# Moving the value products of a query-tile pair behind the next scores in the last batch of a decoder-layer kernel

## The chip, the cores and the metric

One core of one Trainium2 chip runs the whole kernel in one launch. The metric is the device time of that launch in microseconds (us), the median of several executions. The names of the engines in the profile are PE (TensorE, matmuls and transposes), PEld (its weight loads), DVE (VectorE), ACT (ScalarE), POOL (GpSimd) and SP (the engine that only issues transfers here).

## The reference, cut to what matters

```python
x = x + attn(layernorm(x), Wq, bq, Wk, bk, Wv, bv, Wo, bo)   # x: 4 batches x 512 tokens x 512
x = x + experts(layernorm(x), token_ids, ctx)                # 4 experts, each token to one
x = x + ffn(layernorm(x), w_gate, w_up, w_down, ln_weight)   # quantized activations, ternary weights

def attn(h, ...):            # 16 heads of 32, window of 128 keys back, 4 sink keys always seen
    q, k, v = h @ Wq.T + bq, h @ Wk.T + bk, h @ Wv.T + bv
    scores = q @ k.T * 32 ** -0.5
    banned = (j >= 4) & (j < i - 128)      # i query, j key; keys ahead of i are NOT banned
    probs = softmax(where(banned, -inf, scores))
    return (probs @ v) @ Wo.T + bo
```

The change lies in `probs @ v` ("the value products") of the last of the four batches. The computed values stay the same.

## The kernel before, in words

The attention phase works on units (b, g, qt): batch b, a group g of four heads, and one of four query tiles qt of 128 tokens. Group 0 of a batch is worked off at the end of the batch before it, so the last batch (b = 3) has the twelve units g = 1 to 3. Every engine runs its own program, an order written out by hand, and semaphores join them.

For one unit:

- PE, `scores(b, g, qt)` (L948, L956): the products of queries and keys of four heads, in three terms (high and low halves), plus a mask, into the four banks of `s_ps`. There is only one set of these banks, so the scores of a unit wait until ACT has taken all exponentials of the unit before.
- DVE, `maxima` (L724): the row maxima, in two halves of two heads.
- ACT, `exps` (L548): four exponentials with their row sums, the first two after the first half of the maxima, into the buffer `weights[qt]`.
- PE, `transpose_slot(b, g, qt, k)`, k = 0 to 3 (L976; the four sink keys L972; in unit 3 the widened inverse sums L969): the weights are transposed block by block into two banks of `pT_ps`; ACT copies slots 0 and 2 back (L560), DVE slots 1 and 3 (L745, L742). Slot 2 can be transposed when ACT has copied slot 0, slot 3 when DVE has copied slot 1.
- PE, `attend_pair(b, g, pair)` (L998, with L990 for the sinks): for a pair of query tiles (0 and 1, or 2 and 3) the value products, 32 or 24 matmuls and 2 more, into the one bank `pv_ps`.
- DVE, `attn_of(b, g)` (L736): `pv_ps` times the inverse sums, after both pairs of a group; POOL splits the result into a high and a low part (L412, L415), which the output projection needs.

PE's order within a unit is: the scores of the next unit, transposes 0 and 1, a "side" product (projections of Q, K, V or of the output, L889), transposes 2 and 3, and in units 1 and 3 the value products of the pair that is now complete. In the last batch only group 1 has side products (O2, O3, Q3, K3); units (2, 0) to (3, 1) have none, and `o_begun(0)`, the first part of the last output projection, comes in unit (3, 2).

The buffers of both pairs overlap in the memory of `probs`: `weights[3]` lies over a part of `weights[1]`. So the exponentials of unit (g, 3) may not be written before the value products of pair 0 of the group have read `weights[1]`, and those of unit (g + 1, 1) not before the products of pair 2 have read `weights[3]`. Before the change this follows from PE's order, as the scores of those units stand behind the value products.

In what follows a unit is named by (g, qt), all of b = 3, and T0 to T3 are its four sets of transposes.

Of the kernel before, what the change touches and what calls it, by code (L numbers as in the profile page):

```python
# [11 lines left out]
BATCH, SEQ, D = 4, 512, 512  # L12
# [3 lines left out]
HG = HEADS // GH  # L16
# [43 lines left out]
def attention_phase(nc, io, x1, x2, slot_tokens, dense_tokens, sh):  # L60
# [7 lines left out]
    with ExitStack() as ctx:  # L68
# [123 lines left out]
        def width(qt):  # L192
            sink, kts, _ = blocks(qt)
            return SINKS * sink + P * len(kts)
# [21 lines left out]
        def units_before(b, g, qt):  # L216
            return b * GU + g * TT + qt
# [29 lines left out]
        def projected(b, g, qt):  # L247
            name = PROJECTED[g].split()[qt]
            return None if name == "-" or (g and not taken(b, name)) else name
# [9 lines left out]

        def in_key_order(keys):  # L260
            return keys.rearrange("p (u n) -> p u n", u=2)[:, :, SINKS:]

        def key_columns(keys, rows, g, qt):
            if qt < 2:
# [238 lines left out]
        def scalar_program(act):  # L503
# [39 lines left out]

            def exps(b, g, qt, s):
                act.wait_ge(max_ready, units_before(b, g, qt) * 2 + s + 1)
                at = BAND - width(qt) if qt >= 2 else 0
                for h in (2 * s, 2 * s + 1):
                    nc.scalar.activation(weights[qt][:, h, at:at + width(qt)], s_ps[:, h, 0:width(qt)], ACT.Exp,  # L548
                                         bias=neg_max[:, qt % 2, h:h + 1],
                                         accum_out=sums[:, g % 2, qt, h:h + 1]).then_inc(exp_done, 1)  # L550
# [57 lines left out]
        def vector_program(dve):  # L608
# [123 lines left out]

            def attn_of(b, g):
                dve.wait_ge(slot_copied[1], copies_before(b, g, TT - 1, SLOTS - 1) + 1)
                dve.wait_ge(heads_done, b * HG + g + 1)
                nc.vector.tensor_tensor(norm[:], pv_ps[:], norm[:], ALU.mult).then_inc(attn_ready, 1)  # L736

            def copy_slot(b, g, qt, k):
                slot = slots_of(qt)[k]
                dve.wait_ge(slot_transposed, slots_before(b, g, qt, k) + 1)  # L740
                if slot == "rinv":
                    nc.vector.tensor_copy(norm[:], pT_ps[:, 1, :]).then_inc(slot_copied[1], 1)  # L742
                else:
                    a, z = columns(qt, slot)
                    nc.vector.tensor_copy(weights[qt][:, :, a:z], pT_ps[:, 1, :].rearrange("p (h n) -> p h n", h=GH))\  # L745
                        .then_inc(slot_copied[1], 1)

            def unit(b, g, qt, last):
                nxt = (g, qt + 1) if qt + 1 < TT else (g + 1, 0)
                more = not (last and nxt == (HG, 0))  # L750
                coming = b + 1 if g == 0 else b + 2
                prepare = g in (0, HG) and coming < BATCH
                name = turned(b, g, qt - 1) if qt else turned(b, g - 1, TT - 1)
                if name:
                    x_lo(b, int(name[1]), side_ps[:])
                if qt == TT - 1:
                    invert(b, g)
                if (g, qt) == (HG, 0):
                    attn_of(b, g - 1)
                if more:  # L760
                    maxima(b, *nxt, 0)
                    maxima(b, *nxt, 1)
                if qt == 0 and 0 < g < HG:
                    attn_of(b, g - 1)
                if prepare and qt in (1, 2):
                    for t in (2 * qt - 2, 2 * qt - 1):
                        stats_of(coming, t)
                if qt >= 2:
                    a, z = columns(qt, "sink")
                    dve.wait_ge(exp_done, units_before(b, g, qt) * GH + GH)  # L770
                    nc.vector.tensor_reduce(sinks[:], weights[qt][:, :, a:z].unsqueeze(3), AX.X, ALU.max).then_inc(sinks_gathered, 1)
                copy_slot(b, g, qt, 1)
                if prepare and qt in (1, 2):
                    dve.wait_ge(stats_step, coming * TT + 2 * qt)
                    for t in (2 * qt - 2, 2 * qt - 1):
                        variance_of(coming, t)
                name = projected(b, g, qt)
                if name and name[0] == "V":
                    v_of(b if g else -1, int(name[1]), side_ps[:], v_next if g else v_sb)
                if name and name[0] == "O":  # L780
                    dve.wait_ge(side_done, nth(b, name))
                    x1_of(batch_of(b, name), int(name[1]), side_ps[:], side_left)
                copy_slot(b, g, qt, 3)
                if name and name[0] in "QK":
                    qk_lo(heads_of(g, name), name[0], nth_in(b, g, name, "XQK"))
                if prepare and qt == TT - 1:
                    for t in (0, 1):
                        normalize(coming, t)
                if not last and (g, qt) == (1, 0):
                    for t in (2, 3):  # L790
                        normalize(b + 1, t)
                if last and (g, qt) == (HG - 1, TT - 1):

                    e = SPLIT_ORDER[-1]
                    dve.wait_ge(c_split, 2 * EXPERTS - 1)
                    nc.vector.tensor_tensor(place(sh["w_lo"], e), v_next[:], place(sh["w_hi"], e).bitcast(F32), ALU.subtract)\
                        .then_inc(c_split, 1)
                if (g, qt) == (HG, 0):

                    dve.wait_ge(side_left, nth(b, "V3"))  # L800
                    nc.vector.tensor_copy(v_sb[:], v_next[:]).then_inc(v_moved, 1)
# [82 lines left out]
        def tensor_program(pe):  # L884
# [75 lines left out]
            def transpose_slot(b, g, qt, k):  # L960
                slot = slots_of(qt)[k]
                if copies_before(b, g, qt, k):
                    pe.wait_ge(slot_copied[k % 2], copies_before(b, g, qt, k))
                if k == 0:
                    pe.wait_ge(exp_done, units_before(b, g, qt) * GH + GH)
                if slot == "rinv":
                    pe.wait_ge(rinv_widened, b * HG + g + 1)
                    for t in range(TT):
                        last = nc.tensor.transpose(pT_ps[:, 1, place_of(t)], norm[:, t * P:t * P + P], ident[:])  # L969
                elif slot == "sink":  # L970
                    pe.wait_ge(sinks_gathered, 2 * (b * HG + g) + qt - 1)
                    last = nc.tensor.transpose(pT_ps[0:GH * SINKS, 0, 0:P], sinks[:].rearrange("p h n -> p (h n)"), ident[:])  # L972
                else:
                    a, z = columns(qt, slot)
                    for h in range(GH):
                        last = nc.tensor.transpose(pT_ps[:, k % 2, h * P:h * P + P], weights[qt][:, h, a:z], ident[:])  # L976
                last.then_inc(slot_transposed, 1)
# [24 lines left out]
            def attend_pair(b, g, pair):  # L1002
                if pair == 0 and g:
                    pe.wait_ge(attn_ready, b * HG + g)
                    if g == HG:
                        pe.wait_ge(v_moved, b + 1)
                slots = [2, 1, 3, "sink"] if pair else slots_of(pair)
                for n, slot in enumerate(slots):
                    last = attend(b, g, pair, slot, n == 0, n + 1 == len(slots))
                if pair:  # L1010
                    last.then_inc(heads_done, 1)

            def o_begun(t):
                if t == 0:
# [4 lines left out]
            def unit(b, g, qt, last):  # L1019
                nxt = (g, qt + 1) if qt + 1 < TT else (g + 1, 0)  # L1020
                if not (last and nxt == (HG, 0)):
                    scores(b, *nxt)
                transpose_slot(b, g, qt, 0)
                transpose_slot(b, g, qt, 1)
                name = projected(b, g, qt)
                if name:
                    side(b, nth_in(b, g, name), name)
                if last and g == HG - 1 and qt >= 2:
                    o_begun(qt - 2)
                transpose_slot(b, g, qt, 2)  # L1030
                transpose_slot(b, g, qt, 3)
                if last and (g, qt) == (HG - 1, TT - 1):
                    o_begun(2)
                if qt % 2:
                    attend_pair(b, g, qt - 1)
                name = turned(b, g, qt)
                if name:
                    side(b, nth(b, name), name)
# [986 lines left out]
```

## Time and profile before

| | us |
|---|---|
| median of three runs | 785.86 (783.3, 785.86, 787.12) |
| the profiled execution, its own time | 789.38 |
| its span in the trace | 787.3 |
| PE busy | 735.5 (93%) |
| DVE busy | 587.4 (75%) |
| ACT busy | 473.1 (60%) |
| POOL busy | 331.2 (42%) |
| units (1, 0) to (3, 3) and the output projection of the last batch | 378.9 to 457 |

The profiled execution took 2.1 us beyond its span, and 3.5 us more than the median of the runs. Times of rows are counted from the start of the span. The busy share is a mean over stages with different limits: attention reaches to about 457 us, the experts and the feed-forward part follow. The granted clock is given as a share of full speed: 1.00 is 2.4 GHz and 0.50 is 1.2 GHz.

### The profile page before, as it was taken

The page shows a single profiled execution, that of the slowest core. Times are in us where ns is not written, and L with a number is a line of the kernel's source. Part 1 is how long each engine was busy: PE and PEld are TensorE (multiplying, and loading weights), DVE is VectorE, ACT ScalarE, POOL GpSimd, SP SyncE. Part 2 cuts the span into 40 slices and gives each one's busy share as a digit, 9 for nine tenths or more (in the row PEclk, how much of TensorE's full clock was granted, in tenths as well). Part 3 has the DMA queues.
Part 4 walks back from the last instruction along what each step waited for, and adds up shares of the span by engine and source line. Part 5 has one row for each costly group of instructions (what it writes and reads, how often), then busy time and mean ns, then how long its engine had stood idle before and what let it go on. Part 6 is the DMA issues. An engine that isn't in the chain of part 4 may idle for free.

```text
span 787.3 us, 14189 instructions
## 1 busy us (share of the span) xinstructions
PE 735.5 (93%) x5167; PEld 512.7 (65%) x5184; DVE 587.4 (75%) x1099; ACT 473.1 (60%) x1028; POOL 331.2 (42%) x329
## 2 busy tenths in 40 slices
PE   5988999999999999999987989999998999999993
PEld 4866777777777776777764777888874444444441
DVE  6986866886667866766665548878888999999882
ACT  4565666766676665766666314444455787667761
POOL 2011205213242134254553544445546677777661
PEclk9998999999999999999999999999999999999997
DMA  9300012214130322314311356555430233333231
GB/s 314 115 1 27 28 40 95 92 44 151 40 107 29 108 85 77 108 31 153 129 40 55 54 198 258 182 197 201 140 126 25 54 88 87 94 95 102 73 92 42
DMA packets 55474, 78.33 MB, mean 99 GB/s; under 512 B 36335, under 2 KB 38383, under 8 KB 53680
## 3 DMA queue, kind: packets, MB, share of 16 engines
q1 hardware_dynamic: 46336, 51.99, 20.6%
q0 software_dynamic: 8784, 24.93, 9.8%
q8 instruction: 43, 0.70, 0.4%
q10 hardware_dynamic: 288, 0.52, 0.2%
q14 instruction: 23, 0.19, 0.1%
HBM read 56.92 MB, written 17.59 MB: 95 GB/s over the span
## 4 chain that ended last, share of the span: by engine, by line
PE 62%; DVE 20%; issue 8%; ACT 5%; POOL 2%; DMA 1%; another core or an unknown queue 0%; ACTq 0%; SPq 0%; POOLq 0%; DVEq 0%
PE side_ps L889 17%; PE pT_ps L976 10%; PE e_z_ps L1528 7%; PE y_ps L1528 7%; PE pv_ps L998 5%; PE s_ps L948 5%; DVE h L1784 4%; ACT hq L1739 2%; DVE neg_max L724 2%; DVE hw_max L1800 2%; DVE hq_big L1831 2%; PE s_ps L956 2%; PE pT_ps L889 1%; DVE probs L745 1%; ACT f_gate L1746 1%
## 5 line engine op out<-in xcount | busy, mean ns | idle before, releaser
L548 ACT ACTIVATE probs<-s_ps,neg_max 128x512 f32<-128x512 f32 (+2 forms) x256 | 152.5, 611 | 17.9 <-DVE neg_max L724 16.4
L724 DVE TENSOR_REDUCE neg_max<-s_ps 128x2 f32<-128x1024 f32 (+2 forms) x128 | 124.6, 1015 | 36.1 <-PE s_ps L956 35.0
L976 PE MATMUL pT_ps<-ident,probs 128*128 128x128 f32 x832 | 116.5, 282 | 7.8 <-DVE probs L745 7.0
L560 ACT ACTIVATE probs<-pT_ps 128x512 f32<-128x512 f32 x96 | 57.5, 599 | 98.7 <-PE pT_ps L976 97.3
L976 PEld LDWEIGHTS pT_ps<-ident,probs 128*128 128x128 f32 x832 | 95.1, 145 | 23.0 <-DVE probs L745 9.7
L745 DVE COPY probs<-pT_ps 128x512 f32<-128x512 f32 x112 | 76.8, 685 | 39.1 <-PE pT_ps L976 36.2
L1695 POOL TENSOR_TENSOR xg_own<-h,ln_w_sb 128x512 f32<-128x512 f32 x63 | 81.9, 1308 | 37.9 <-DVE h L1784 37.8
L889 PE MATMUL side_ps<-w_hi 128*128 128x512 f32 x172 | 71.0, 413 | 0.0
L412 POOL TENSOR_TENSOR aT_hi<-norm,one_col 128x512 fp32r<-128x512 f32 x15 | 15.6, 1041 | 126.6 <-DVE norm L736 88.4
L889 PE MATMUL side_ps<-w_hi,w_lo 128*128 128x512 f32 x172 | 67.5, 392 | 0.0
L889 PE MATMUL side_ps<-w_lo,w_hi 128*128 128x512 f32 x172 | 67.0, 390 | 0.0
L1739 ACT ACTIVATE hq<-hq_big,minus_offset 128x1024 bf16<-128x1024 f16 x30 | 32.9, 1142 | 37.3 <-DVE hq_big L1831 37.3
L998 PE MATMUL pv_ps<-probs,v_sb 128*32 128x256 f32 (+1 forms) x896 | 54.0, 378 | 1.4 <-DVE probs L745 0.9
L1905 PE MATMUL y_ps<-w_tern,hqT 128*128 128x512 bf16 x210 | 54.5, 379 | 0.7
L404 POOL TENSOR_TENSOR norm<-rinv,one_col 128x512 f32<-128x512 f32 x16 | 16.7, 1041 | 86.0 <-DVE rinv L731 86.0
L548 ACT ACTIVATION_READ_ACCUMULATOR probs<-s_ps,neg_max 128x1 f32 x256 | 52.8, 206 | 0.0
L1657 PE MATMUL e_xT_ps<-w_tern,xqT_home 128*128 128x512 bf16 x126 | 32.6, 378 | 7.3 <-DVE h L1784 6.5
L1800 DVE TENSOR_REDUCE hw_max<-xg_own 128x1 f32<-128x1024 f32 x32 | 38.7, 1209 | 0.1
L998 PEld LDWEIGHTS pv_ps<-probs,v_sb 128*32 128x32 f32 x896 | 25.7, 112 | 20.0 <-issue 8.0
L889 PEld LDWEIGHTS side_ps<-w_hi,w_lo 128*128 128x128 f32 x172 | 32.3, 188 | 7.4
L1905 PEld LDWEIGHTS y_ps<-w_tern,hqT 128*128 128x128 bf16 x224 | 21.4, 98 | 23.4
L889 PEld LDWEIGHTS side_ps<-w_hi 128*128 128x128 f32 x172 | 32.4, 188 | 5.9 <-DVE k_lo L648 0.4
(290 smaller groups left out, 1779.4 us busy)
## 6 DMA issues: line engine op xcount, KB each, us to landing
w_piece<-w_ffn SPq DMA_DIRECT2D x24, 512.0 KB
w_stage<-w_ffn SPq DMA_DIRECT2D x12, 1024.0 KB
xres<-x POOLq DMA_DIRECT2D x4, 1024.0 KB, 6.4
xn<-x SPq DMA_DIRECT2D x3, 1024.0 KB
x<-xres POOLq DMA_DIRECT2D x3, 1024.0 KB, 4.8
xn<-c SPq DMA_DIRECT2D x2, 1024.0 KB, 5.1
v_next<-c SPq DMA_DIRECT2D x2, 1024.0 KB, 7.5
xn<-x SPq DMA_DIRECT2D x4, 256.0 KB, 3.4
```

Of the source, the lines that this page charges most:

```text
L548: nc.scalar.activation(weights[qt][:, h, at:at + width(qt)], s_ps[:, h, 0:width(qt)], ACT.Exp, bias=neg_max[:, qt % 2, h:h + 1], accum_out ...
L560: nc.scalar.activation(out, turned_p, ACT.Identity).then_inc(slot_copied[0], 1)
L724: nc.vector.tensor_reduce(neg_max[:, qt % 2, 2 * s:2 * s + 2], s_ps[:, 2 * s:2 * s + 2, 0:width(qt)], AX.X, ALU.max, negate=True).then_inc ...
L745: nc.vector.tensor_copy(weights[qt][:, :, a:z], pT_ps[:, 1, :].rearrange("p (h n) -> p h n", h=GH))\
L889: last = nc.tensor.matmul(out, lt, r, start=(first and n == 0), stop=(final and n == len(terms) - 1))
L976: last = nc.tensor.transpose(pT_ps[:, k % 2, h * P:h * P + P], weights[qt][:, h, a:z], ident[:])
L998: last = nc.tensor.matmul(pv_ps[HD * h:HD * h + HD, to], v_sb[:, slot, f:f + HD], p, start=first, stop=final, tile_position=(0, HD * h))
L1528: last = nc.tensor.matmul(out, lt[:, k, :], r[:, at, :], start=(n == 0), stop=(n == 3 * DK - 1))
L1695: nc.gpsimd.tensor_tensor(hw[:, t % 2, c, :], h[:, t % 2, c, :], ln_w[:, c * CHK:c * CHK + CHK], ALU.mult)\
L1739: nc.scalar.activation(hq[:, cols], hq_code[:, cols], ACT.Identity, bias=minus_offset[:]).then_inc(hq_packed, 1)
L1800: nc.vector.tensor_reduce(hw_max[:, i, n:n + 1], flat(hw, i)[:, n * HALF:n * HALF + HALF], AX.X, ALU.max, apply_absolute_value=True).then_ ...
L1905: last = nc.tensor.matmul(sums_of(t), hqT[:, t % 2, k, :], down_w[:, k, :], start=(k == 0), stop=(k == FK - 1))
```

## The change

In the last batch, for groups 1 to 3, the value products of a pair no longer stand at the end of the unit that completes the pair. They stand one unit later: behind the scores of the unit after that and behind T0 and T1. This holds for five pairs: (1, pair 0), (1, pair 2), (2, pair 0), (2, pair 2) and (3, pair 0). The pair (3, pair 2) stays at the end. Two waits are added on ACT, since PE's order no longer protects the overlapping buffers; DVE takes `attn_of` of groups 1 and 2 behind the copy of slot 1. `heads_done` now counts both pairs, in all batches.

```diff
+        def values_late(b, g, pair):
+            return b == BATCH - 1 and 1 <= g < HG and (g, pair) != (HG - 1, 2)
+
+        def values_of(b, g, pair):
+            return 2 * (b * HG + g) + (2 if pair else 1)
...
             def exps(b, g, qt, s):
                 act.wait_ge(max_ready, units_before(b, g, qt) * 2 + s + 1)
+                if s == 0 and qt == 3 and values_late(b, g, 0):
+                    act.wait_ge(heads_done, values_of(b, g, 0))
+                if s == 0 and qt == 1 and g and values_late(b, g - 1, 2):
+                    act.wait_ge(heads_done, values_of(b, g - 1, 2))
...
-                dve.wait_ge(heads_done, b * HG + g + 1)
+                dve.wait_ge(heads_done, values_of(b, g, 2))
...
-                if qt == 0 and 0 < g < HG:
+                follows_late = qt == 0 and 0 < g < HG and values_late(b, g - 1, 2)
+                if qt == 0 and 0 < g < HG and not follows_late:
                     attn_of(b, g - 1)
...
                 copy_slot(b, g, qt, 1)
+                if follows_late:
+                    attn_of(b, g - 1)
...
-                if pair:
-                    last.then_inc(heads_done, 1)
+                last.then_inc(heads_done, 1)
...
                 transpose_slot(b, g, qt, 0)
                 transpose_slot(b, g, qt, 1)
+                if qt == 2 and values_late(b, g, 0):
+                    attend_pair(b, g, 0)
+                if qt == 0 and g and values_late(b, g - 1, 2):
+                    attend_pair(b, g - 1, 2)
...
-                if qt % 2:
+                if qt % 2 and not values_late(b, g, qt - 1):
                     attend_pair(b, g, qt - 1)
```

## Rows read from the trace of the kernel before

**Rows 1.** The page: busy time and share of the span by engine.
```profile
PE 735.5 (93%) x5167; PEld 512.7 (65%) x5184; DVE 587.4 (75%) x1099; ACT 473.1 (60%) x1028; POOL 331.2 (42%) x329
```
**Rows 2.** Busy time by stretch: length, engines' busy us (instructions), granted clock, DMA.
```profile
378.90:401.30 22.40, 22.40 (x189) 17.65 (x186) 15.12 (x22) 13.81 (x39) 7.50 (x6) 1.00 0.29 97
...
409.40:412.80 3.40, 3.40 (x18) 2.81 (x15) 2.51 (x3) 2.44 (x8) 3.40 (x2) 0.51 0.00 0
...
419.60:423.00 3.40, 1.56 (x17) 0.97 (x10) 3.03 (x4) 2.44 (x6) 0.84 (x1) 1.00 0.00 0
423.00:426.40 3.40, 3.40 (x32) 1.77 (x32) 0.69 (x1) 1.59 (x6) 0.00 (x0) 0.50 0.03 5
...
433.20:436.60 3.40, 3.40 (x18) 2.82 (x16) 2.49 (x3) 2.42 (x8) 3.40 (x2) 0.50 0.00 0
```
**Rows 3.** Chain that ended last, in order of time: start, length, what.
```profile
391.96 0.88 PE pT_ps L976 x8
...
401.35 1.22 PE pv_ps L998 x24
...
403.19 0.69 PE s_ps L948 x8
...
409.47 3.51 PE pT_ps L976 x16
412.98 1.95 PE pv_ps L998 x32
414.93 0.56 PE s_ps L948 x8
415.49 0.33 PE s_ps L956 x4
...
418.74 0.14 issue
418.88 1.00 PE s_ps L948 x9
...
419.90 2.35 DVE neg_max L724 x2
...
422.98 1.11 PE pT_ps L969 x4
424.09 2.29 PE pv_ps L998 x24
```
**Rows 4.** Timeline of ACT: start, length, line, out<-in, idle before and releaser.
```profile
401.38 0.21 ACT L548 ACTIVATION_READ_ACCUMULATOR probs<-s_ps,neg_max 128x1 f32 x1
...
405.39 0.69 ACT L548 ACTIVATE probs<-s_ps,neg_max 128x512 f32<-128x512 f32 x1
...
410.36 0.60 ACT L560 ACTIVATE probs<-pT_ps 128x512 f32<-128x512 f32 x1 [1.70 <-PE pT_ps L976]
410.86 0.58 ACT L548 ACTIVATE probs<-s_ps,neg_max 128x388 f32<-128x388 f32 x1
...
413.00 0.22 ACT L548 ACTIVATION_READ_ACCUMULATOR probs<-s_ps,neg_max 128x1 f32 x1
...
416.79 0.47 ACT L548 ACTIVATE probs<-s_ps,neg_max 128x260 f32<-128x260 f32 x1
...
421.16 0.69 ACT L548 ACTIVATE probs<-s_ps,neg_max 128x512 f32<-128x512 f32 x1
...
429.24 0.69 ACT L548 ACTIVATE probs<-s_ps,neg_max 128x512 f32<-128x512 f32 x1
```
**Rows 5.** Timeline of PE: the same columns.
```profile
407.74 0.66 PE L976 MATMUL pT_ps<-ident,probs 128*128 128x128 f32 x4 [1.75 <-DVE probs L745]
408.32 0.45 PE L948 MATMUL s_ps<-k_hi,q_hi 32*128 32x388 f32 x4
...
438.67 0.39 PE L948 MATMUL s_ps<-k_hi,q_hi 32*128 32x260 f32 x4
```
**Rows 6.** Timeline of POOL: the same columns.
```profile
432.13 1.28 POOL L415 TENSOR_TENSOR aT_lo<-norm,aT_hi 128x512 fp32r<-128x512 f32 x1
```

## The prediction, on record before the result

> **What bounds the kernel now.** I read the page first: PE is busy for 93% of the span [rows 1], so a gain can only come where PE pauses or runs slow. Then I cut the last batch into stretches [rows 2]. Until 401.3 us, with the side products of group 1, PE has no pause: reordering its work there gains nothing. From group 2 on there are no side products, and PE pauses (1.56 us busy out of 3.40 in one stretch). In three stretches the granted clock is 0.50, that is 1.2 GHz. Each comes after a passage in which PE paused, the first after a pause of 1.75 us [rows 2, 5].
>
> Then I read the chain of waits [rows 3] beside ACT's timeline [rows 4] for the round from unit (2, 1) to (3, 1). It is a ring: scores on PE, first half of the maxima on DVE, four exponentials on ACT, and then the next scores, since the score banks exist once. Its first exponentials start at 405.39 in one round and at 429.24 in the next: 23.85 us. The value products interrupt the ring twice in it: 412.98 to 414.93 (pair 0) and from 424.09 (pair 2), where 24 matmuls take 2.29 us at the low clock against 1.22 us at 401.35 at the full one. The question is what the ring becomes when these products stand elsewhere.
>
> **The links of the ring**, from row starts at full clock [rows 3 to 5]:
> - From the first exponential of a unit to the next scores: 512 columns, 408.32 - 405.39 = 2.93; 260 columns, 418.88 - 416.79 = 2.09; 388 columns, the last sum read ends at 413.22, 2.36 after 410.86, plus the hop of 0.14: 2.50.
> - Scores alone: 260 columns, 414.93 to 415.82, 0.9; when they start from a pause 0.07 more (0.96). 512 columns without a mask 1.00, with a mask about 1.25 from a pause (four mask matmuls add 0.2 to 0.3). 388 columns 409.47 - 408.32 = 1.15.
> - From scores of 512 columns to the exponentials: 421.16 - 419.90 = 1.26. T0 and T1 together: 0.88. Value products: 403.19 - 401.35 = 1.84 for pair 2, 1.95 for pair 0 (1.9 used).
> - Where ACT's copy of slot 0 stands between (units with 388 columns): T0 0.44 and copy 0.50 behind the scores.
>
> **What is removed and added.** Nothing is computed less. Removed from the place before the scores are the products of five pairs. What they are moved past are the scores (0.9 to 1.25) and T0 and T1 (0.88); they issue no transfers, and SP's and POOL's queues aren't touched. The catch is the added wait on ACT: the exponentials of (g, 3) and (g + 1, 1) must wait for the same products. The old path at such a place is products, scores, maxima (or copy), exponentials. The new one is scores, T0, T1, products, exponentials. The products stay on the path; the maxima go off it, and T0 and T1 come on it. Behind the waiting exponentials on ACT stand the copy of slot 2, on which the last transposes depend, and behind their end the next scores, the ring itself. So:
>
> - Place (1, pair 0): inside the stretch without pauses. Exponentials of (1, 3) wait for products that end where they began by work before. 0.
> - Place (1, pair 2): old 405.39. New: the scores of (2, 1) can't start when PE is free at 401.35, since the exponentials of (2, 0) end at 401.59; plus the hop, 401.74. Then 1.25 + 0.88 + 1.84 + 0.02: exponentials at about 405.75. Late by 0.36.
> - (2, 1): scores at 405.75 + 2.93 = 408.68, end 409.83, T0 and copy 0.97: exponentials at 410.82 (old 410.86, where T0 and T1 ran at the low clock).
> - Place (2, pair 0): scores of (2, 3) at 410.82 + 2.50 = 413.32 instead of 414.93. They are early by 1.6. But then 0.96 + 0.88 + 1.9 + 0.02 = 3.76 gives exponentials at 417.08, old 416.79: late by 0.3.
> - (3, 0): 417.08 + 2.09 + 1.02 + 1.26 = 421.45, old 421.16.
> - Place (2, pair 2): scores of (3, 1) at 421.45 + 2.93 = 424.38, plus 1.25 + 0.88 + 1.84 + 0.02 = 3.99: 428.37 against the old 429.24. Early by 0.87, and only because the old place ran at the low clock (0.55 in L969, 1.07 in the 24 matmuls).
> - Group 3: 428.37 + 2.93 + 2.12 (1.15 + 0.97, scores, T0 and copy) + 2.50: scores of (3, 3) at 435.92, old 438.67 [rows 5], early by 2.75; the products (1.9) now follow them before `o_begun(0)`. PE is early by about 0.8 there, and from that point on its work is dense and the same, so 0.8 is what arrives at the end of attention.
>
> Sum with PE at full clock throughout: -0.8 us. The old round lost about 2.4 to the low clock (0.55 and 1.07 in (2, 3), some 0.4 each at the first transposes of (2, 1) and (3, 1)); against an old ring at full clock the new one would be slower by about 1.6. The moved order costs a little by itself.
>
> The small parts. `attn_of` behind DVE's copy of slot 1 lets T3 of (2, 0) start earlier (old pause 1.75 us [rows 5]), but scores could start at 408.32 anyway, when ACT was done: 0, covered by the exponentials. POOL's split, ending at 433.41 [rows 6], moves with `attn_of` and is wanted by `o_begun(0)` only after the products of (3, pair 0), near 439.7: covered by over 5 us. The waits on ACT: no row shows a second wait alone; from 0 to the hop of 0.14 [rows 3] at four binding places, so 0 to 0.6; I take 0.1, as the trace's hops between engines that are ready are mostly a few hundredths. The sixteen added semaphore increments are 0: the scores at 403.19 follow directly on products that already carry one [rows 3]. The Trainium skill ("TensorE: Matmul & The Clock Gate", "The cost: per-tile semaphore tail") gives about 26 ns for each increment; an estimate by that page is 16 x 0.026 = 0.4 us if every one lay on the path, and the row at 403.19 shows none of it.
>
> **The clock in the new order.** The new order still has pauses, worked out from the same links: about 1.6 us before the scores of (2, 2), in place of 1.75; about 1.5 and 0.6 around the sink transposes of (2, 3) and 0.65 before the scores of (3, 1), where before 1.56 us of work out of 3.40 preceded a fall; about 2 us before the scores of (3, 2). So falls will follow as before. What they hit is different: behind the pauses of (2, 3) stand scores, T0, T1 and products in a row, 3.97 us, all on the path. A low stretch was 3.4 us long in each of three cases [rows 2] and does half the work, so it costs up to 1.7; for a part cover I take 1.4. The falls at (2, 1) and (3, 1) hit T0 in front of a copy: 0.43 each (T0 once more). The low estimate for all is 0, the high one three times 1.7. I take the fall at (2, 3) and one of the others: 1.4 + 0.4. The Trainium skill (the same page, "Part 1: The HAM clock gate") says that the point at which the clock changes varies between runs of one kernel; the three times from 783.3 to 787.12 don't contradict that, and no run here shows its cause.
>
> **Sum**: -0.8 + 0.1 + 1.4 + 0.4 = +1.1 us. The profiled execution's own 789.38 would become 790.5. It lies 3.5 above the median of the runs, so I carry the difference over: 785.86 + 1.1, about 787.0. Half a per cent, 3.9 us, is what a measurement of this kernel can tell from no change, so this is no change.
>
> **The rivals.**
> 1. Break-even as summed, with falls of the clock in old or new places: between -0.8 and +2.7 (a second place at 1.7). Chance 0.72.
> 2. PE stays warmer: no fall in the last batch, and PE's work overlaps more than my links say (up to 0.3 at four places): -0.8 - 1.2 = -2.0, 783.9. For it: the densest work is pushed together. Against it: the sum of pauses hardly shrinks. Chance 0.15.
> 3. The products go under the maxima entirely, the added wait never binds: four places (all but the first) at 1.84 to 1.95, 7.6 us faster, 778.3. It decides if T0, T1 and the products, 2.72 us, fit into the 1.26 us of the maxima. By the rows they don't. Chance 0.05; this is where "faster" has its chance.
> 4. Slower: the low clock covers the new row of scores, transposes and products at each of the three places after a pause, 3 x 1.7 = 5.1, and the increments and waits cost too: -0.8 + 5.1 + 0.6 = +4.9, 790.8. It decides from three such falls on. For it: the path through PE at such a place is now 3.97 us instead of products and scores of 2.8. Against it: in front of (2, 2)'s and (3, 2)'s units the pauses are shorter or the fall comes one unit too early. Chance 0.08.
>
> The range takes rivals 1, 2 and most of 4, and adds the scatter of a median of few runs (the three lie 3.8 us apart): 783.5 to 790.0. The chances by the bound of half a per cent: faster 0.05, same 0.87, slower 0.08.
>
> **What the profile after would show.** Right: exponentials of (2, 1), (2, 3), (3, 1) and (3, 3) released by PE's value products and no longer by the maxima; the maxima of those units done 1.5 us before; scores of (2, 3) and (3, 3) starting 1.6 to 2.8 us earlier while the exponentials behind them don't; the round from (2, 1) to (3, 1) between 22.5 and 24.5 us. Wrong: if exponentials follow the maxima directly, if the round is below 21.5, or if a pause of PE appears before 401 us. A difference above 4 us with an unchanged round would mean that the cause lies outside the last batch.

## The result, and the profile after

The changed kernel takes 787.02 us, the kernel before 785.26 us, both medians of 20 runs. The ratio of all runs but one is 1.0026, with a 95% interval from 1.0014 to 1.0039: 2.0 us slower, between 1.1 and 3.1 (the two medians alone differ by 1.8). One run of the changed kernel took 1477.61 us, at a granted clock on record as 1.000; it is left out of the ratio, and its cause is open. By the bound of half a per cent this is no change; by its own interval it is a small loss. Forecast was 787.0.

The profiled execution took 786.93 us, with a span of 785.0, and is so 2.3 us shorter in its span than that of the kernel before. That says nothing of the change: the first exponential of (1, 2), before which PE has the same order in both programs, starts at 382.43 here and started 3.2 us later there. A part of these 3.2 us is a further fall of the clock far ahead of the change: from 57.0 to 61.5 us the granted clock was 0.62 on the mean before and 1.00 after; both have one near 68 us. From that exponential to the first sum of the output projection out of the score banks on DVE (`x1_of`, the row `xres<-s_ps`) it is 452.73 - 382.43 = 70.30 us after, and was 69.51 us before. I call this length **the stage** below; both ends lie outside what the change moves. Behind the stage all profiled executions of this document but one (e7) agree within 0.3 us, 332.0 to 332.3; ahead of it they scatter from 382.1 to 385.6.

The page of after, engines' busy time, against [rows 1]; PE is less busy because its clock fell less often in this execution:

```profile
PE 730.8 (93%) x5167; PEld 509.5 (65%) x5184; DVE 587.1 (75%) x1099; ACT 473.4 (60%) x1028; POOL 330.7 (42%) x329
```

The timeline of ACT of after, the first exponentials of the four units behind a moved pair (the columns of [rows 4]):

```profile
402.75 0.69 ACT L559 ACTIVATE probs<-s_ps,neg_max 128x512 f32<-128x512 f32 x1 [1.74 <-PE pv_ps L1004]
...
413.94 0.48 ACT L559 ACTIVATE probs<-s_ps,neg_max 128x260 f32<-128x260 f32 x1 [1.79 <-PE pv_ps L1012]
...
426.81 0.69 ACT L559 ACTIVATE probs<-s_ps,neg_max 128x512 f32<-128x512 f32 x1 [2.66 <-PE pv_ps L1004]
...
438.01 0.48 ACT L559 ACTIVATE probs<-s_ps,neg_max 128x260 f32<-128x260 f32 x1 [1.79 <-PE pv_ps L1012]
```

All four are now released by PE's value products: (2, 1), (2, 3), (3, 1) and (3, 3). This is the added wait, and it binds each time. The round from (2, 1) to (3, 1) takes 426.81 - 402.75 = 24.06 us, where [rows 4] give 23.85.

The chain that ended last, of after, over the same places as [rows 3]:

```profile
382.34 2.80 PE side_ps L903 x12
...
387.78 1.86 PE pv_ps L1012 x32
389.64 2.94 PE side_ps L903 x12
...
398.63 0.96 PE s_ps L962 x11
399.59 0.33 PE s_ps L970 x4
399.92 0.88 PE pT_ps L990 x8
400.81 1.22 PE pv_ps L1012 x24
402.02 0.64 PE pv_ps L1004 x2
...
410.11 0.63 PE s_ps L962 x11
410.74 0.33 PE s_ps L970 x4
411.07 0.88 PE pT_ps L990 x8
411.95 1.91 PE pv_ps L1012 x32
...
421.14 0.99 PE s_ps L962 x9
422.14 0.52 PE s_ps L970 x4
422.66 1.71 PE pT_ps L990 x8
424.37 1.72 PE pv_ps L1012 x24
426.09 0.64 PE pv_ps L1004 x2
...
426.81 2.79 ACT probs L559 x8
```

Three times the same row of work stands in front of the exponentials: scores, two sets of transposes, value products, all on PE. At (2, 3) it is 413.94 - 410.11 = 3.83 us; 3.76 was worked out. At (2, 1) it is 402.75 - 398.63 = 4.12 us; the same row at (3, 1), from 421.14, takes 5.67 us, because the transposes took 1.71 instead of 0.88, the 24 matmuls 1.72 instead of 1.22 and the mask's matmuls 0.52 instead of 0.33. The stretches of after say why (the columns of [rows 2]); in the last batch of this execution the clock fell once, right behind a passage in which PE was busy 1.78 us out of 3.40:

```profile
418.60:422.00 3.40, 1.78 (x17) 1.00 (x17) 2.17 (x4) 3.14 (x10) 0.00 (x0) 0.99 0.00 0
422.00:425.40 3.40, 3.40 (x32) 2.53 (x32) 2.91 (x3) 0.60 (x1) 0.00 (x0) 0.51 0.02 5
```

So the two profiled executions can't be set against each other as they are: before had three falls in the last batch, after one. What both programs would take without falls is what the experiments had to show.

### The profile page after: what moved, and what is told of

Same layout as the page of the kernel before. It is cut to its first block, busy times and chain, and to the rows that moved or that the text cites. A ratio compares the mean times of both kernels' runs of the same rounds, so it can differ in the third digit from the quotient of the medians.

```text
span 785.0 us, 14194 instructions
## 1 busy us (share of the span) xinstructions
PE 730.8 (93%) x5167; PEld 509.5 (65%) x5184; DVE 587.1 (75%) x1099; ACT 473.4 (60%) x1028; POOL 330.7 (42%) x329
## 4 chain that ended last, share of the span: by engine, by line
PE 61%; DVE 16%; ACT 10%; issue 8%; POOL 2%; DMA 1%; ACTq 0%; SPq 0%; POOLq 0%; DVEq 0%
PE side_ps L903 17%; PE pT_ps L990 9%; PE e_z_ps L1545 7%; PE y_ps L1545 7%; PE pv_ps L1012 6%; PE s_ps L962 5%; DVE h L1801 3%; ACT probs L559 3%; ACT sq_junk L1771 2%; ACT hq L1756 2%; ACT f_gate L1763 2%; DVE hq_big L1848 2%; DVE neg_max L735 2%; PE s_ps L970 2%; PE pT_ps L903 1%
## 5 line engine op out<-in xcount | busy, mean ns | idle before, releaser
L990 PE MATMUL pT_ps<-ident,probs 128*128 128x128 f32 x832 | 114.4, 278 | 6.1 <-DVE probs L756 5.3
L990 PEld LDWEIGHTS pT_ps<-ident,probs 128*128 128x128 f32 x832 | 93.4, 143 | 20.9 <-DVE probs L756 7.5
L1012 PE MATMUL pv_ps<-probs,v_sb 128*32 128x256 f32 (+1 forms) x896 | 52.3, 370 | 0.0
L962 PE MATMUL s_ps<-k_hi,q_hi 32*128 32x512 f32 (+2 forms) x256 | 33.8, 456 | 6.5 <-ACT probs L559 6.5
```

The costliest lines, as they stand in the source:

```text
L962: last = nc.tensor.matmul(s_ps[:, h, 0:width(qt)], q[rows, g % HG, cols], key_columns(k, rows, g % HG, qt), start=(n == 0), stop=(n == 2 a ...
L1012: last = nc.tensor.matmul(pv_ps[HD * h:HD * h + HD, to], v_sb[:, slot, f:f + HD], p, start=first, stop=final, tile_position=(0, HD * h))
```

## The experiments

Theory 1, **the ring**: with the buffers overlapping, the exponentials wait for products that now stand behind scores, T0 and T1, so nothing leaves the path and a little is added. Rival A: the waits, the added increments and DVE's order cost the time. Rival B: only the clock's falls, which lie elsewhere in the new order, make the difference. "Extra" in the table stands for small products without use that keep PE busy; they come with e7 below.

In the table all distances are in us between first exponentials on ACT, read from the timeline of ACT as above; "falls" is the number of low stretches of PE's clock from 400 us to the end of attention in the profiled execution. A distance marked with * has at least a part of a fall in it.

| kernel | ratio to before (95%) | (2,0) to (2,1) | (2,2) to (2,3) | (3,0) to (3,1) | stage | falls |
|---|---|---|---|---|---|---|
| before | 1 | 6.58 | 5.93* | 8.08* | 69.51 | 3 |
| after | 1.0026 (1.0014 to 1.0039) | 6.96 | 6.25 | 8.50* | 70.30 | 1 |
| e1 waits only | 0.9988 (0.9976 to 1.0000) | 6.59 | 5.93* | 6.51 | 68.00 | 1 |
| e2 pair 0 late | 1.0024 (1.0010 to 1.0038) | 6.58 | 6.26 | 8.13* | 71.07 | 2 |
| e3 pair 2 late | 1.0012 (0.9999 to 1.0024) | 6.96 | 6.42* | 8.23* | 69.97 | 3 |
| e4 apart | 0.9961 (0.9946 to 0.9976) | 5.71 | 4.36 | 5.32 | 64.22 | 0 |
| e5 T1 behind | 0.9978 (0.9965 to 0.9991) | 6.52 | 5.82 | 6.52 | 67.35 | 0 |
| e6 split, shared | 0.9930 (0.9909 to 0.9951) | 6.17 | 5.14 | 5.46 | 64.45 | 0 |
| e7 after, ten extra | 1.0038 (1.0025 to 1.0052) | 6.96 | 6.25 | 6.96 | 70.08 | 0 |
| e8 apart, extra | 0.9934 (0.9912 to 0.9955) | 5.71 | 4.35 | 5.33 | 64.22 | 0 |
| e9 before, extra | 0.9979 (0.9967 to 0.9991) | 6.58 | 5.94 | 6.53 | 67.21 | 0 |
| e10 after, five extra | 0.9999 (0.9987 to 1.0011) | 6.95 | 6.26 | 6.96 | 68.78 | 0 |
| e11 split, apart | 0.9933 (0.9917 to 0.9948) | 6.20 | 4.53 | 5.47 | 64.16 | 0 |

**e1, the waits without the move.** All of the change but PE's order.

```diff
-                if qt == 2 and values_late(b, g, 0):
-                    attend_pair(b, g, 0)
-                if qt == 0 and g and values_late(b, g - 1, 2):
-                    attend_pair(b, g - 1, 2)
...
-                if qt % 2 and not values_late(b, g, qt - 1):
+                if qt % 2:
```

> PE's order is that of the kernel before; the two waits on ACT, the increment of heads_done for both pairs in all batches, and attn_of behind DVE's copy of slot 1 are those of the change. Theory 1 (the ring: what costs is the new row scores, T0, T1, value products in front of the exponentials): no difference, within 0.8 us of before. Rival A (the waits, increments and DVE's order cost the 2 us): about 2 us slower, 1.0025.

Not slower: 0.9988, that is 0.9 us faster (0 to 1.9) where at most 0.8 of difference was expected, and where no fall lies in either the distances are those of before to 0.01 us (7.31, 5.87 and 6.59 from (1, 2) on). Rival A falls. The sixteen increments, which this kernel carries, cost nothing that can be measured. The Trainium skill ("TensorE: Matmul & The Clock Gate", "The cost: per-tile semaphore tail") would allow up to 0.4 us by the prediction's estimate; the interval's upper end is 1.0000, and nothing in these runs points to such a cost, though their falls, which vary from run to run, are in the interval too. And e1 gave the first look at (3, 0) to (3, 1) in the old order without a fall: 6.51 us instead of 8.08.

**e2 and e3, one half of the move each.**

```diff
-            return b == BATCH - 1 and 1 <= g < HG and (g, pair) != (HG - 1, 2)
+            return b == BATCH - 1 and 1 <= g < HG and pair == 0          # e2
+            return b == BATCH - 1 and 1 <= g < HG - 1 and pair == 2      # e3
```

> Only the value products of pair 0 of groups 1 to 3 stand late. Theory 1: at places (2, pair 0) and (3, pair 0) the exponentials come 0.3 to 0.4 us later after the previous exponentials than in the old order at full clock, and each first product behind value products starts up to 0.2 later: +0.8 to +1.2 us in all, 1.0010 to 1.0015. In the trace the time from the first exponential of (2, 2) to that of (2, 3) is 6.25, as after. Rival A: about +1.2. Rival B (only falls of the clock make the difference): anything from -1 to +3, with every link at full clock equal to before.

> Only the value products of pair 2 of groups 1 and 2 stand late. Theory 1: +0.4 at (1, pair 2) and +0.4 at (2, pair 2), +0.8 us in all, 1.0010; from the first exponential of (3, 0) to that of (3, 1) 6.9 us at full clock and up to 8.6 with a fall in it. Rival A: about +0.8. Rival B: no fixed sign.

e2: 1.0024, more than the 1.0015 I had as the upper end, though its interval reaches below that. (2, 2) to (2, 3) is 6.26 as in after, +0.33 on the old order, and (3, 2) to (3, 3) is 6.25, with 5.93 in e1; of the places of pair 2, (2, 0) to (2, 1) is unchanged at 6.58, and the other has a fall in it as before. The runs of e2 have a median granted clock of 0.986 where those of before have 0.988, so a part of its excess may be falls. e3: 1.0012, with +0.38 at (2, 0) to (2, 1); its 6.42 at (2, 2) to (2, 3), where the old order stands, has a fall in it. The parts together (3.6 per thousand) are not distinguishable from the whole (2.6), given intervals of 1.2 to 1.4 to either side. By its distances each half loses by itself (e3's ratio alone, from 0.9999 on, doesn't show it): there is no good half that the other spoils. The profiled executions of these two had two and three falls, so their stages can't be used.

**e4, the buffers apart.** The order of after; the second pair gets its own 6 KB for each partition, and the waits on ACT, no longer needed, go.

```diff
-        probs = sb("probs", [P, 2 * GH * SEQ + GH * BAND])
+        probs = sb("probs", [P, 2 * GH * (SEQ + BAND)])
...
-                2: probs[:, 2 * GH * (SEQ - BAND // 2):].rearrange("p (u h n) -> p u h n", u=2, h=GH)}
+                2: probs[:, 2 * GH * SEQ:].rearrange("p (u h n) -> p u h n", u=2, h=GH)}
...
-                if s == 0 and qt == 3 and values_late(b, g, 0):
-                    act.wait_ge(heads_done, values_of(b, g, 0))
-                if s == 0 and qt == 1 and g and values_late(b, g - 1, 2):
-                    act.wait_ge(heads_done, values_of(b, g - 1, 2))
```

> The order of the change, but the buffers of the two pairs no longer overlap (6 KB more for each partition), so the two waits on ACT are gone: nothing makes the exponentials wait for the value products. Theory 1: the products leave the ring at four places; exponentials follow the maxima or the copy of slot 0 again; about 3 us faster than before (0.996), 5 us faster than after. Rival A: at most 1 us from after. Rival B: near after. If PE itself is the bound of the last batch, it is not faster than before either.

0.9961, 3.1 us faster than before and 5 faster than after, as expected. This is the experiment that decides: the same order on PE and DVE gains as soon as the exponentials need not wait. In its chain around (3, 1) the maxima stand in front of the exponentials again, and no value products stand in the ring between them:

```profile
418.49 0.97 PE s_ps L958 x11
419.46 0.23 PE s_ps L966 x2
419.69 0.02 issue
419.71 1.24 DVE neg_max L731
420.95 0.02 issue
420.97 2.79 ACT probs L555 x8
423.77 0.04 issue
423.81 0.80 PE s_ps L958 x9
```

The gain is 3 us and not the 7.6 of rival 3, and the distances show why. At four places it is 6.58 - 5.71, twice 5.93 - 4.36 (the second from (3, 2) to (3, 3), 4.35) and 6.52 - 5.32 (e9 for the old order without a fall), 5.2 us in all, since part of the old products already ran before the ring was ready for the next scores. About 0.2 is lost around group 1, where PE has no pauses, and 0.25 at (2, 3) to (3, 0). And at the end 2 us are given back: the exponentials of (3, 3) start at 430.26, but PE's first product of the output projection only at 431.96, 1.7 behind them, where it starts 0.3 ahead of them before. PE has become the bound there.

**e5, T1 behind the products.**

```diff
                 transpose_slot(b, g, qt, 0)
-                transpose_slot(b, g, qt, 1)
                 if qt == 2 and values_late(b, g, 0):
                     attend_pair(b, g, 0)
                 if qt == 0 and g and values_late(b, g - 1, 2):
                     attend_pair(b, g - 1, 2)
+                transpose_slot(b, g, qt, 1)
```

> As after, but the value products stand between T0 and T1 instead of behind both. Theory 1: one set of four transposes (0.44 us) leaves the ring at each of the four places: from the first exponential of (2, 2) to that of (2, 3) 5.8 instead of 6.25, from (2, 0) to (2, 1) 6.5 instead of 6.96; in all 1.8 us faster than after, 1.0003 of before. Rival B (the clock alone): no fixed change of these distances at full clock.

The distances came out as worked out, 5.82 and 6.52: 0.43 and 0.44 less than after. The chain of e5 at (2, 3) has one set of transposes left in front of the products:

```profile
409.61 0.64 PE s_ps L962 x10
410.24 0.33 PE s_ps L970 x4
410.57 0.44 PE pT_ps L990 x4
411.01 1.91 PE pv_ps L1012 x32
...
413.00 1.96 ACT probs L559 x8
```

By its stage (67.35) this kernel is near the old order without falls (67.21, e9). The measured 0.9978 is better than the 1.0003 expected, by about the 1.6 us that falls cost the kernel before (e9). Its profiled execution had no fall in the last batch, and the granted clocks of its twelve runs say that this was no luck: their median is 0.9925, near the 0.992 and 0.993 of the filled kernels e9 and e10, where before and after have 0.988. Why this order has fewer falls isn't shown.

**e7, e9 and e10, the clock held.** Extra products of the identity with itself (the expectations call them transposes) into the unused side bank, results not used, in PE's pauses, in after with ten (e7) and five (e10) for each pause, in before with five or two (e9). The comments in the diff are not in the code; where they name e9, its line differs.

```diff
+            def fill(n):
+                pe.wait_ge(side_left, nth(BATCH - 1, "K3"))
+                for _ in range(n):
+                    nc.tensor.matmul(side_ps[:, 0:P], ident[:], ident[:], start=True, stop=True)
...
+                if last and (g, qt) in ((2, 0), (2, 2), (3, 0)):   # e7, e10: behind T3; e9: (2, 0) and (3, 0) behind T2
+                    fill(10)                                       # e10: 5
...
+                if last and (g, qt) == (2, 3):                     # behind T1; e9: also fill(2) at (2, 2)
+                    fill(10)                                       # e10: 5
```

> As after, with ten extra transposes of the identity (results unused) in each of four pauses of PE in units (2, 0), (2, 2), (2, 3) and (3, 0), so that the clock has less reason to fall. Theory 1: no fall in the last batch; from (3, 0) to (3, 1) 6.9 us instead of 8.5, the other distances as after; 1 to 2 us faster than after, 1.000 to 1.0015 of before. If the distances other than (3, 0) to (3, 1) shrink, the price of the order itself is a matter of the clock and theory 1 is wrong.

> The kernel before, with extra transposes of the identity into the unused side bank in PE's pauses of the last batch: five behind T2 of (2, 0) and (3, 0), two behind T1 of (2, 2), five behind T1 of (2, 3), short enough to end within the pauses. Theory 1: no fall of the clock in the last batch; all distances at their full-clock lengths (6.59, 4.94, 5.93, 4.37, 6.51, 4.94, 5.93 us from the first exponential of (2, 0) on); 1 to 2 us faster than before, 0.998. If the falls cost nothing on the path, 1.000.

> As e7 with five extra transposes for each pause instead of ten, which ran past the pauses there. Theory 1: no fall, distances 6.96, 4.94, 6.25, 4.37, 6.96, 4.94, 6.25 us; 1.7 to 2.0 us slower than e9, about 1.000 of before. Rival B (the clock alone makes the difference of the change): the same time as e9.

e7 missed its time: 1.0038 instead of about 1.001. The clock indeed never fell in its last batch and (3, 0) to (3, 1) is 6.96, but I had sized the filling wrongly: each of the ten is two records of 0.12 us, so a row of ten takes 2.4 us, longer than any pause. The timeline of PE of e7, with the scores of (2, 2) directly behind:

```profile
405.12 2.40 PE L1029 MATMUL side_ps<-ident 128*128 128x128 f32 x20
407.45 0.45 PE L962 MATMUL s_ps<-k_hi,q_hi 32*128 32x388 f32 x4
```

That cost 0.48 at (2, 1) to (2, 2), 0.6 at (2, 3) to (3, 0) and 0.25 at (3, 1) to (3, 2), 1.3 in all. It isn't the whole miss: e7 is 3.1 us slower than e10 by the ratios. Its profiled execution also has 335.7 us behind the stage instead of 332.0 to 332.3, with a fall of the clock near 770 us; why is open, and so is whether its other runs have that. With five, e10 has after's distances everywhere, 68.78 us of stage; e9 has before's, 67.21 (two of its other distances are 0.1 longer than in e1, 5.05 for 4.94, which is its filling). From the timelines of ACT, (3, 0) and (3, 1) in e9 and then in e10:

```profile
417.99 0.69 ACT L548 ACTIVATE probs<-s_ps,neg_max 128x512 f32<-128x512 f32 x1
...
424.52 0.69 ACT L548 ACTIVATE probs<-s_ps,neg_max 128x512 f32<-128x512 f32 x1
```

```profile
417.96 0.69 ACT L559 ACTIVATE probs<-s_ps,neg_max 128x512 f32<-128x512 f32 x1
...
424.92 0.69 ACT L559 ACTIVATE probs<-s_ps,neg_max 128x512 f32<-128x512 f32 x1 [1.74 <-PE pv_ps L1004]
```

The order alone, at full clock, costs 68.78 - 67.21 = 1.57 us by the trace, and 0.9999 - 0.9979, 1.6 us, by the runs. Without e9's own 0.2 us of filling it would be about 1.8 by the trace. Rival B is out as the sole cause. The runs give the price of the falls too, each with an error of about 1 us or more: before loses 1.6 us to them (e9 against before, 0.7 to 2.6), after about 2.1 (0.9999 against 1.0026).

The granted clock, on record for every run as a mean over its span, counts the falls where no trace was kept. One low stretch of 3.4 us lowers it by about 0.0022 (an estimate: half of 3.41 us out of 785). The medians are 0.988 in 22 runs of before and 0.988 in the 19 of after, 0.992 in e9 and 0.993 in e10. So an ordinary run of either order has about two low stretches more than the filled kernels, and neither order has clearly more than the other.

**e6, e8 and e11, versions that beat both.** e6 keeps the shared buffers and cuts each pair's products by slots, so that those whose weights are ready go into PE's pauses; e8 is e4 with the filling in its one pause; e11 is e6 with e4's buffers.

```diff
+                if qt == 2 and values_late(b, g, 0):            # behind T0
+                    attend_pair(b, g, 0, slice(2, 4))
+                if qt == 0 and g and values_late(b, g - 1, 2):
+                    attend_pair(b, g - 1, 2, slice(3, 4))
...
+                if qt == 3 and g > 1 and values_late(b, g, 2):  # behind T1
+                    attend_pair(b, g, 2, slice(0, 2))
...
+                if qt == 1 and values_late(b, g, 0):            # behind T2
+                    attend_pair(b, g, 0, slice(0, 1))
...
+                if qt == 1 and values_late(b, g, 0):            # behind T3
+                    attend_pair(b, g, 0, slice(1, 2))
+                if qt == 3 and values_late(b, g, 2):
+                    attend_pair(b, g, 2, slice(2 if g > 1 else 0, 3))
```

> The buffers still overlap, and the value products are cut up by slots: those whose weights are copied early go into PE's pauses (slot 0 of pair 0 between T2 and T3 of unit 1, slot 1 behind T3; slots 2 and 1 of pair 2 behind T1 of unit 3, slot 3 behind T3), the rest stands behind the next scores and T0 (slots 2 and 3 of pair 0; for pair 2 only the sinks, so no wait is left there). (1, pair 0) stands as before. Theory 1: from (2, 2) to (2, 3) 4.9 us, from (3, 0) to (3, 1) 5.5, from (2, 0) to (2, 1) about 6.0; about 3.3 us faster than before, 0.996. If it isn't, then the count of products in front of the exponentials is not what sets the ring.

> As e4 (buffers apart, no wait on ACT), with ten extra transposes of the identity in the one pause of 1.6 us that PE still has, in unit (2, 3). Theory 1: the same distances as e4, and no fall in any run: between 0 and 1 us faster than e4, 0.995 to 0.996 of before, and less scatter.

> e6 with the buffers apart and without the last wait on ACT. Theory 1: from (2, 2) to (2, 3) 4.4 us instead of 5.14, from (3, 0) to (3, 1) as in e6; 0.8 us faster than e6, half a us faster than e4, 0.992 to 0.995 of before.

All three are at 0.993, 5.2 to 5.5 us faster than before. e6's distances were worked out as 4.9, 5.5 and 6.0 and are 5.14, 5.46 and 6.17. Its chain at (2, 3) shows eight and sixteen value products, in two parts of 0.57 and 1.04 us, where 1.9 us stood in one place:

```profile
410.06 0.57 PE pv_ps L1010 x8
410.63 0.56 PE s_ps L960 x9
411.19 0.33 PE s_ps L968 x4
411.52 0.44 PE pT_ps L988 x4
411.97 1.04 PE pv_ps L1010 x16
```

Of its 5.5 us, 2.8 are the shorter stage at full clock (67.21 - 64.45), and about 1.6 are falls that it seems to be spared; 1.1 are left over, inside the interval (3.3 us in all had been expected). That its runs are spared falls fits their median granted clock of 0.992. e8's stage is e4's to 0.01 us; its intervals and e4's overlap, so whether the filling helped is not shown, though the median granted clock is 0.992 in e8 and 0.990 in e4: e4's profiled execution without a fall was better than its ordinary ones. e11 was expected 0.8 us under e6 and is the same: its stage is only 0.3 shorter, though (2, 2) to (2, 3) fell to 4.53. PE is near its bound at the end of the batch in both (busy for 15.79 of the 16 us from 430 to 446 in either), and the distances won ahead of it are lost there. e6, which needs no memory, is the one to keep.

## Why the prediction was right

**The path, link by link.** The step that carried the prediction, products in front of the exponentials by way of the added wait, is shown by the four releasers after and by e4. The links from [rows 3 to 5] predicted distances that no trace had shown: (2, 0) to (2, 1) 0.36 longer than before, measured 0.38; (2, 2) to (2, 3) 6.26, measured 6.25; (3, 0) to (3, 1) 6.92, measured 6.96 (e10).

**The order's own cost.** The forecast's -0.8, the new order without falls against the profiled execution of before, came out as 68.78 - 69.51 = -0.73. The 1.6 us against an old order at full clock came out as 1.57, with some luck: place (1, pair 0) was put at 0 and cost 0.18 (5.88 to 6.02 and 7.30 to 7.34 in e9 and e10), which e9's filling of 0.2 hides again.

**The clock.** The term that was mis-sized is the old order's falls. I summed against the profiled execution, whose three falls cost its stage about 2.3 us (69.51 - 67.21), and then carried the sum over to the median as if it had the same. The runs lose 1.6 by the ratio (0.7 to 2.6). The granted clocks point the same way: the profiled execution had 0.983, lower than each of the 22 runs of before on record (0.984 to 0.990), and about two low stretches more than their median, some of them ahead of the last batch. On the new side I took 1.8 and the runs say 2.1. With these the sum is 1.57 - 1.6 + 2.1 = 2.1 us; this is no test of it, since the last two are differences of the same ratios whose sum is the measured 2.0, and only the 1.57 comes from the traces by itself. Nor is the distance from the forecast 1.1 to the measured 2.0 (1.1 to 3.1) clear of noise. The one fall of after cost 8.50 - 6.96 = 1.5 on the path, where 1.4 was taken; the second fall, taken at 0.4, did not come in the profiled execution.

**The small parts.** The waits, increments and DVE's order at 0.1: nothing measurable in e1. The maxima of (2, 3), (3, 1) and (3, 3) were done 1.6, 2.0 and 1.6 us before the exponentials, as forecast (1.5), but those of (2, 1) only 0.15 before. From 376.7 to 398.3 us of after PE is busy for the whole 21.6 us, so no pause appeared in group 1, as said.

**The rivals.** Rival 2 (a warmer PE makes it faster) did not come: even with no fall at all, e10 is not faster than before. Rival 3 needed the wait not to bind; e4 made it so by other buffers, and the gain was 3 us and not 7.6, for the reason given there. Rival 4, three falls in the new row, was not in the one profiled execution of this order without filling. A single run of 790.97 among the twenty shows that such times occur; its granted clock, 0.978, is the lowest of all and means about four to five low stretches more than the median, where in the kernel is not known.

## What to carry to other kernels

Moving work behind the next stage's start takes it off the path only if nothing that the next stage writes waits for it: look at which buffers overlap, and give them room or move only the parts whose buffers are free, before changing the order. Where a ring of three engines sets the pace, add up its links from row starts in one execution; they predicted whole rows moved to a new place to 0.05 us, and the cut-up products of e6 to 0.24. And before comparing two profiled executions, count the stretches of low clock in each, in the whole span, and take the price of the order from a pair of kernels in which the clock doesn't fall.

## What the runs showed of the hardware

A row of full-size products behind value products (32-column tiles) took longer than the same row behind transposes: the side product of twelve 2.94 us at 389.64, and 2.80 at 382.34. Distances between events of the ring came out the same in different executions to 0.02 us where the clock did not fall, while whole runs scattered by 4 to 5 us. The clock fell to 0.50 for 3.4 us behind stretches without any long pause: the longest single one was 1.60 us ahead of the fall of after, and 1.60 to 1.75 ahead of the three of before. Short rows of extra products in the pauses were enough to leave no low stretch in the last batch of the profiled executions of e9 and e10, and cost at most 0.2 us.
